# Weights of layers 1 and 2 laid out by partition and both loaded at the front, tile 0's rows written from ACT's queue, layer 2's mixed weights made earlier on DVE

## The chip, the cores and the metric

The kernel runs on one core of a Trainium2 chip. The metric is the device time of one execution in microseconds (us). A core has five engines with their own instruction streams: PE (TensorE, matmul), DVE (VectorE), ACT (ScalarE), POOL (GpSimd) and SP (SyncE, used here for DMA issues only). Sixteen DMA engines move data between HBM (the chip's memory) and SBUF (128 partitions). PSUM is the memory that PE writes.

## The reference, cut to what matters

For 512 samples, 39 embedding rows of 16 numbers each are gathered, and three layers of a "compressed interaction network" are computed on them, followed by a small dense tower.

```python
e = stack([tbl_f[ids[:, f]] for f in range(39)], axis=1)         # (512, 39, 16)
prev = e
for k in range(3):                                               # 128 units each
    h = prev.shape[1]                                            # 39, then 128, 128
    z = einsum('bmd,bhd->bdmh', e, prev).reshape(b, D, m * h)
    t = einsum('bdc,co->bdo', z, w[k]) + bias[k]
    t = transpose(t, (0, 2, 1))
    t = t / sqrt(sum(t * t, axis=(-2, -1), keepdims=True))
    logit.append(t); prev = t
z = sum(concatenate(logit, axis=1), axis=-1)                     # (512, 384)
h = concatenate([z, dense_ctx], axis=1)
h = maximum(h @ W_top1 + b_top1, 0)
h = maximum(h @ W_top2 + b_top2, 0)
y = h @ W_top3
```

w[1] and w[2] have 128 * 39 rows of 128 numbers (2.56 MB each); row m * 128 + h belongs to field m and unit h.

## The kernel before, in words

**Tiling.** The batch is cut into 16 tiles of 32 samples; a tile's data are 32 * 16 = 512 columns. Tile 0 is written out with `first=True`, tiles 1 to 14 are a loop, tile 15 is written out with `last=True`.

**Data path of a tile.** POOL gathers the embedding rows with ten indirect DMAs (L300) into `gathered`. Three DMAs (`write_rows`) write them to `xt` in HBM, where the data have one row per field. POOL also makes `mixed` from them (L316 to L321), and `write_mixed` writes it to `xq` in HBM. From `xt` come `x3` and `xr` (117 partitions, layer 0: `load_x` and `load_shifted`, four groups g of `xr`), and from `xt` and `xq` comes `xb`, whose rows are repeated over all 128 partitions (`load_chunk`).

**Layer 0.** DVE multiplies `x3` (in tile 0 from SBUF, in the others from a copy in PSUM that ACT makes in `copy_x`) into `xr` (`products0`, L625), and PE multiplies with `w0_sb` (L799).

**Layers 1 and 2.** The 39 fields are worked through in 11 chunks c = 0 to 10 (`CHUNKS`). Four are direct chunks "D" (c = 0, 2, 7, 10) with 2 or 3 fields: DVE makes `z` = t * xb (L642) and PE multiplies with the fields' weights (L808). Seven are pair chunks "P" with two pairs of fields: a scheme of the Strassen kind, in which PE makes seven half-size products per pair (L822) instead of eight. It needs sums of parts of `z`, made by POOL (L337, L340) and for two chunks (c = 5 and 6 of layer 1) by DVE (L655) from a copy that ACT makes, and sums of parts of the weights. These "mixed weights" `s_sb[k]` are made once per layer by `mixed_weights(k, part)` on DVE (L612) in four parts, each of a 128x768 and a 128x128 instruction. Part 3 overwrites a quarter of `w_sb[k]` in place. PE waits for all four parts before chunk 0 of the layer in tile 0.

**What sets the order.** Everything is ordered by hand: each engine has one stream, and semaphores hold it. `z` is a ring, so that DVE waits for PE to have used a slot (`z_used`) before it writes it again. Within a tile DVE runs the products of layer 1, c = 0 to 10, then `shared_sums` and `add_shared` (the end of layer 1), then the products of layer 2. PE runs layer 1, layer 0 of the next tile, layer 2. In the loop's tiles DVE makes the next tile's `products0` after chunks 9 and 10 of layer 1 (L745 to L748); in tile 0 it makes them after all of layer 1's chunks (L749 to L753), with parts 1 to 3 of layer 2's mixed weights behind them, and part 0 ahead of chunk 10 (L743).

**The queue of SP.** SP issues, in this order: the small inputs, w0b, w0a, w1 (L372); then the writes of tile 0's rows (`write_rows(0)`), `xq` of tile 0, two of the four groups of `xr`; when all four have landed, the chunk loads of tile 0; in their middle (after c = 5) the writes of tile 1's rows and of `xq` of tile 1; then w2 (L430) and the layer 0 loads of tile 1. ACT's queue issues `x3` and the other two groups of `xr` of tile 0. The lines of the weight loads:

```python
sp.dma_start(w_sb[1][:, :, :], w1.rearrange("(m h) o -> h m o", h=P)).then_inc(w_loaded[1], 16)   # L372
sp.dma_start(w_sb[2][:, :, :], w2.rearrange("(m h) o -> h m o", h=P)).then_inc(w_loaded[2], 16)   # L430
```

Each partition h gets 39 pieces of 512 B, one per field.

Of the kernel before, what the change touches and what calls it, by code (L numbers as in the profile page):

```python
# [127 lines left out]
def build(nc, ids_in, base_in, masks_in, table, xt, xq, dense_t, w0a, w0b, w1, w2, b0, b1, b2,  # L128
          wt1, bt1, wt2, bt2, wt3, out):
    ctx = ExitStack()  # L130
    with ctx:
# [148 lines left out]

        block = ctx.enter_context(nc.Block())
# [84 lines left out]
        def _(sp):  # L366
# [5 lines left out]
            sp.dma_start(w_sb[1][:, :, :], w1.rearrange("(m h) o -> h m o", h=P)).then_inc(w_loaded[1], 16)  # L372

            def write_rows(i):

                def write(first, g0, g1, fields=GROUP):
                    blk = xt[bass.ds(i, 1), first:first + (g1 - g0 - 1) * GROUP + fields, :].rearrange(
                        "a (g f) (b d) -> (a f b) g d", f=fields, d=EMB)
                    sp.dma_start(blk, gathered[0:fields * TILE_B, g0:g1, :]).then_inc(xt_written, 16)

                sp.wait_ge(rows_gathered, 16 * (GROUPS - 1) * (i + 1))
                write(0, 0, GROUPS - 1)
                write(FIELDS, 0, (XT_ROWS - FIELDS) // GROUP)
                sp.wait_ge(last_gathered, 16 * (i + 1))
                write((GROUPS - 1) * GROUP, GROUPS - 1, GROUPS, LAST_GROUP)
# [28 lines left out]
            write_rows(0)  # L414
# [9 lines left out]
            for c in range(NCH):  # L424
                load_chunk(0, c)
                if c == NCH // 2:

                    write_rows(1)
                    write_mixed(1)
            sp.dma_start(w_sb[2][:, :, :], w2.rearrange("(m h) o -> h m o", h=P)).then_inc(w_loaded[2], 16)  # L430
            sp.wait_ge(xt_written, 96)
            sp.wait_ge(acc0_ready, 1)
            load_layer0(1)

# [7 lines left out]
            with sp.Fori(1, TILES - 1) as i:  # L442
                load_fields(i)
                write_rows(i + 1)
# [24 lines left out]
        def _(act):  # L469
# [5 lines left out]

            act.wait_ge(xt_written, 48)
# [112 lines left out]
        def _(dve):  # L589
# [143 lines left out]
            def tile(i, first=False, last=False):  # L733
                for c in range(NCH):
# [39 lines left out]
            products0(0, range(len(LOADS0)))  # L774
# [205 lines left out]
```

## Time and profile before

| what | us |
|---|---|
| device time, median of 3 runs | 1170.16 (1168.98 to 1170.77) |
| device time of the profiled execution | 1173.38 |
| its span, from the first to the last instruction | 1171.6 |
| busy in the span: PE | 1120.3 (96%) |
| DVE | 994.8 (85%) |
| POOL | 946.5 (81%) |
| ACT | 144.6 (12%) |
| mean granted TensorE clock | 0.991 |

Spans and starts are counted in us from the first instruction. A timeline row has the start, the length, the engine (SPq and ACTq: a DMA issue on that queue; PEld: a weight load of PE), the line, the operation, output<-inputs with buffer numbers left out, the form and the count of instructions merged; in brackets stands the idle time of the engine before it and what ended it ("issue": nothing that the profile shows). A window row has the length, then busy time and instruction count of each engine asked for, the granted clock (1.00 is 2.4 GHz, 0.50 is 1.2 GHz), the mean busy share of the 16 DMA engines, and GB/s. Ends of matmuls are modelled, and a share can come out a little above 1.

### The profile page before, as it was taken

The page shows a single profiled execution, that of the slowest core. Times are in us where ns is not written, and L with a number is a line of the kernel's source. Part 1 is how long each engine was busy: PE and PEld are TensorE (multiplying, and loading weights), DVE is VectorE, ACT ScalarE, POOL GpSimd, SP SyncE. Part 2 cuts the span into 40 slices and gives each one's busy share as a digit, 9 for nine tenths or more (in the row PEclk, how much of TensorE's full clock was granted, in tenths as well). Part 3 has the DMA queues.
Part 4 walks back from the last instruction along what each step waited for, and adds up shares of the span by engine and source line. Part 5 has one row for each costly group of instructions (what it writes and reads, how often), then busy time and mean ns, then how long its engine had stood idle before and what let it go on. Part 6 is the DMA issues. An engine that isn't in the chain of part 4 may idle for free. (4 is left out here: it accounts for less than half of the span.)

```text
span 1171.6 us, 22368 instructions
## 1 busy us (share of the span) xinstructions
PE 1120.3 (96%) x8252; PEld 612.8 (52%) x8252; DVE 994.8 (85%) x875; ACT 144.6 (12%) x298; POOL 946.5 (81%) x646
## 2 busy tenths in 40 slices
PE   0788999999999999999999999999999999999999
PEld 0344555555555555555555555555555555555553
DVE  2658989899898989989898998988999898999782
ACT  0001111101111110111111011111101011110102
POOL 5566889798888979898897989889798988958680
PEclk9898999999999999999999999999999999999999
DMA  6886637293653718275472827547282844728010
GB/s 181 252 273 222 200 104 265 67 320 92 241 181 127 251 65 328 75 261 161 143 245 68 318 71 270 152 152 247 72 303 71 284 138 168 236 69 300 1 51 1
DMA packets 102345, 205.81 MB, mean 176 GB/s; under 512 B 49915, under 2 KB 52923, under 8 KB 102326
## 3 DMA queue, kind: packets, MB, share of 16 engines
q1 hardware_dynamic: 95312, 203.29, 51.7%
q0 software_dynamic: 5120, 1.29, 1.1%
q10 hardware_dynamic: 1894, 0.96, 0.4%
q8 instruction: 13, 0.21, 0.1%
q14 instruction: 6, 0.05, 0.0%
HBM read 203.05 MB, written 2.46 MB: 175 GB/s over the span
## 5 line engine op out<-in xcount | busy, mean ns | idle before, releaser
L642 DVE TENSOR_TENSOR z<-t_ps,xb 128x2048 f32<-128x2048 f32 (+2 forms) x352 | 711.1, 2043 | 68.0 <-PE acc L822 43.5
L340 POOL TENSOR_TENSOR sums<-z,sums 128x1024 f32<-128x1024 f32 x224 | 531.6, 2373 | 53.8 <-DVE sums L655 38.7
L808 PE MATMUL acc<-z,w_sb 128*64 128x512 f32 x1408 | 327.6, 601 | 16.5 <-DVE z L642 10.7
L822 PE MATMUL mix_ps<-sums,s_sb 128*64 128x256 f32 x1792 | 330.8, 380 | 2.0 <-POOL sums L340 0.8
L337 POOL TENSOR_TENSOR sums<-z 128x512 f32<-128x512 f32 x192 | 245.7, 1280 | 83.6 <-DVE z L642 79.4
L822 PE MATMUL acc<-z,w_sb 128*64 128x256 f32 x896 | 269.4, 383 | 0.2
L822 PE MATMUL mix_ps<-z,w_sb 128*64 128x256 f32 x896 | 269.4, 383 | 0.0
L822 PE MATMUL acc<-z,s_sb 128*64 128x256 f32 x896 | 267.9, 381 | 0.0
L822 PE MATMUL p_ps<-z,w_sb 128*64 128x256 f32 x896 | 267.9, 381 | 0.0
L822 PEld LDWEIGHTS mix_ps<-sums,s_sb 128*64 128x64 f32 x1792 | 187.2, 137 | 99.3 <-POOL sums L340 13.5
L822 PE MATMUL acc<-sums,w_sb 128*64 128x256 f32 x896 | 230.9, 380 | 0.0
L808 PEld LDWEIGHTS acc<-z,w_sb 128*64 128x64 f32 x1408 | 104.5, 138 | 176.6 <-issue 159.7
L300 POOL DMA_INDIRECT gathered<-in_table,rows_of x160 | 154.0, 962 | 52.6 <-issue 35.7
L822 PEld LDWEIGHTS acc<-z,w_sb 128*64 128x64 f32 x896 | 121.6, 138 | 106.3 <-issue 56.1
L822 PEld LDWEIGHTS acc<-z,s_sb 128*64 128x64 f32 x896 | 123.5, 138 | 61.2 <-issue 1.1
L799 PE MATMUL acc<-xr,w_sb 117*64 117x512 f32 x448 | 103.2, 612 | 28.9 <-DVE xr L625 28.1
L822 PEld LDWEIGHTS p_ps<-z,w_sb 128*64 128x64 f32 x896 | 123.4, 138 | 0.0
L822 PEld LDWEIGHTS mix_ps<-z,w_sb 128*64 128x64 f32 x896 | 121.6, 138 | 0.0
L822 PEld LDWEIGHTS acc<-sums,w_sb 128*64 128x64 f32 x896 | 120.7, 137 | 0.0
L799 PEld LDWEIGHTS acc<-xr,w_sb 117*64 117x64 f32 x448 | 33.7, 141 | 94.9 <-issue 94.6
L625 DVE TENSOR_TENSOR xr<-t_ps,xr 117x1024 f32<-117x1024 f32 (+1 forms) x60 | 62.5, 1082 | 1.4 <-issue 1.3
L525 ACT COPY cross<-mix_ps 64x256 f32<-64x256 f32 x32 | 11.7, 365 | 394.5 <-PE acc L822 264.3
(80 smaller groups left out, 447.7 us busy)
## 6 DMA issues: line engine op xcount, KB each, us to landing
xb<-xt SPq DMA_DIRECT2D x128, 512.0 KB, 6.5
xb<-xq SPq DMA_DIRECT2D x112, 512.0 KB, 5.1
xb<-xt SPq DMA_DIRECT2D x48, 768.0 KB, 6.8
xr<-xt SPq DMA_DIRECT2D x47, 468.0 KB
x<-xt SPq DMA_DIRECT2D x15, 234.0 KB
xr<-xt SPq DMA_DIRECT2D x15, 234.0 KB
gathered<-in_table,rows_of POOLq DMA_INDIRECT x160
xt<-gathered SPq DMA_DIRECT2D x16, 72.0 KB, 2.3
```

The source lines that it names most:

```text
L300: nc.gpsimd.indirect_dma_start(gathered[0:n, g, :], None, table[:, :], bass.IndirectOffsetOnAxis(rows_of[0:n, g:g + 1], 0)).then_inc(rows_ ...
L337: nc.gpsimd.tensor_tensor(t2, t3, b11, ALU.add).then_inc(pool_t2, 1)
L340: nc.gpsimd.tensor_tensor(t41, b2, t2_twice, ALU.subtract).then_inc(t41_ready, 1)
L525: nc.scalar.copy(cross[RIGHT, N2], mix_ps[LEFT, N2]).then_inc(cross_ready, 1)
L625: nc.vector.tensor_tensor(xr[:, k0:k1, :], x.rearrange("p (a n) -> p a n", a=1).broadcast_to([WIDE, k1 - k0, N]), xr[:, k0:k1, :], ALU.mul ...
L642: nc.vector.tensor_tensor(z[:, at:at + n, :], t_ps[k - 1][:, :].rearrange("p (a n) -> p a n", a=1).broadcast_to([P, n, N]), xb[:, XB_ROW[c ...
L799: last = nc.tensor.matmul(acc0[o, :], w0_sb[:, k, o], xr[:, k, :], start=(k == 0), stop=(k == STEPS0 - 1))
L808: last = nc.tensor.matmul(acc[k][o, :], w_sb[k][:, field + r, o], z[:, at + r, :], start=(c == 0 and r == 0), stop=(c == NCH - 1 and r == ...
L822: return nc.tensor.matmul(bank[side, cols], weights, moving, start=start, stop=stop, skip_group_check=True)
```

## The change

- The host lays w1 and w2 out by unit: 128 rows (one per partition) of 39 * 128 numbers, 19,968 B in one piece. The plain copy of them in SBUF is what it was.
- SP issues w1 and w2 one behind the other at the front.
- `write_rows` becomes a function of the queue. Tile 0's three row writes are issued by ACT, in front of its wait for them; the later tiles' by SP as before.
- On SP, `write_mixed(1)` moves from the middle of tile 0's chunk loads to behind the layer 0 loads of tile 1.
- On DVE, layer 2's mixed weights: parts 0 and 1 between the first and the second group of tile 0's `products0`, part 2 after chunk 3 and part 3 after chunk 4 of layer 1 in tile 0.
- On DVE, tile 1's `products0` stand after chunks 9 and 10 of tile 0 as in every other tile.

```diff
+        def write_rows(engine, i):
...
+                engine.dma_start(blk, gathered[0:fields * TILE_B, g0:g1, :]).then_inc(xt_written, 16)
...
-            sp.dma_start(w_sb[1][:, :, :], w1.rearrange("(m h) o -> h m o", h=P)).then_inc(w_loaded[1], 16)
...
+            sp.dma_start(w_sb[1][:, :, :], w1).then_inc(w_loaded[1], 16)
+            sp.dma_start(w_sb[2][:, :, :], w2).then_inc(w_loaded[2], 16)
...
-            write_rows(0)
             write_mixed(0)
...
                 if c == NCH // 2:
 
-                    write_rows(1)
-                    write_mixed(1)
-            sp.dma_start(w_sb[2][:, :, :], w2.rearrange("(m h) o -> h m o", h=P)).then_inc(w_loaded[2], 16)
+                    write_rows(sp, 1)
             sp.wait_ge(xt_written, 96)
             sp.wait_ge(acc0_ready, 1)
             load_layer0(1)
+            write_mixed(1)
...
+            write_rows(act, 0)
             act.wait_ge(xt_written, 48)
...
-                    if c == NCH - 2 and first:
-                        mixed_weights(2, 0)
-                    if c == 9 and not first and not last:
+                    if first and c in (3, 4):
+                        mixed_weights(2, c - 1)
+                    if c == 9 and not last:
                         products0(i + 1, (0, 1, 2,))
-                    if c == 10 and not first and not last:
+                    if c == 10 and not last:
                         products0(i + 1, (3,))
-                if first:
-
-                    products0(i + 1, range(len(LOADS0)))
-                    for part in range(1, 4):
-                        mixed_weights(2, part)
...
-            products0(0, range(len(LOADS0)))
+            products0(0, (0,))
+            for part in range(2):
+                mixed_weights(2, part)
+            products0(0, range(1, len(LOADS0)))
...
+    def by_unit(w):
+        return np.ascontiguousarray(w.reshape(FIELDS, UNITS, UNITS).transpose(1, 0, 2))
...
-        "w1": a["L0_rec_w1"], "w2": a["L0_rec_w2"], "b0": a["L0_rec_b0"], "b1": a["L0_rec_b1"],
+        "w1": by_unit(a["L0_rec_w1"]), "w2": by_unit(a["L0_rec_w2"]), "b0": a["L0_rec_b0"], "b1": a["L0_rec_b1"],
```

DVE's stream at the end of layer 1 in tile 0, before: chunks 8 and 9 (L642), part 0 of the mixed weights (L612), chunk 10, `products0` of tile 1 (L625), parts 1 to 3, and the first of `shared_sums` (L663).

```order
L642 TENSOR_TENSOR z<-t_ps,xb 128x2048 x2
L612 TENSOR_TENSOR s_sb<-w_sb 128x768
L612 TENSOR_TENSOR s_sb<-w_sb 128x128
L642 TENSOR_TENSOR z<-t_ps,xb 128x1536
L625 TENSOR_TENSOR xr<-t_ps,xr 117x1024 x3
L625 TENSOR_TENSOR xr<-t_ps,xr 117x512
L612 TENSOR_TENSOR s_sb<-s_sb,w_sb 128x768
L612 TENSOR_TENSOR s_sb<-s_sb,w_sb 128x128
L612 TENSOR_TENSOR s_sb<-w_sb,s_sb 128x768
L612 TENSOR_TENSOR s_sb<-w_sb,s_sb 128x128
L612 TENSOR_TENSOR w_sb<-w_sb 128x3x4x64
L612 TENSOR_TENSOR w_sb<-w_sb 128x2x64
```

The same place of DVE in the changed kernel:

```order
L642 TENSOR_TENSOR z<-t_ps,xb 128x2048 x2
L625 TENSOR_TENSOR xr<-t_ps,xr 117x1024 x3
L642 TENSOR_TENSOR z<-t_ps,xb 128x1536
L625 TENSOR_TENSOR xr<-t_ps,xr 117x512
L663 TENSOR_TENSOR cross<-cross,mix_ps 64x256
```

Chunk 10 has three instructions of `products0` ahead of it instead of one part of the mixed weights, and nothing of the mixed weights is left at this place. Parts 2 and 3 stand further up in the changed kernel, behind chunk 3 and behind chunk 4 (the first row here is chunk 3, the last is chunk 5):

```order
L642 TENSOR_TENSOR z<-t_ps,xb 128x2048
L612 TENSOR_TENSOR s_sb<-w_sb,s_sb 128x768
L612 TENSOR_TENSOR s_sb<-w_sb,s_sb 128x128
L642 TENSOR_TENSOR z<-t_ps,xb 128x2048
L612 TENSOR_TENSOR w_sb<-w_sb 128x3x4x64
L612 TENSOR_TENSOR w_sb<-w_sb 128x2x64
L642 TENSOR_TENSOR z<-t_ps,xb 128x2048
```

SP's queue from the middle of tile 0's chunk loads on, before (`xb` is a chunk load, L379 the row writes of tile 1, L390 its `xq`, L430 w2, L273 and L279 the layer 0 loads of tile 1):

```order
L379 DMA xt<-gathered 96x16
L390 DMA xq<-mixed 128x4x16
L401 DMA xb<-xq 128x1024
L401 DMA xb<-xt 128x1024
L401 DMA xb<-xt 128x1536
L401 DMA xb<-xq 128x1024
L401 DMA xb<-xt 128x1024
L401 DMA xb<-xq 128x1024
L401 DMA xb<-xt 128x1024
L401 DMA xb<-xt 128x1536
L430 DMA w_sb<-in_w 128x39x128
L273 DMA x<-xt 117x1x512
```

The same place in the changed kernel (`xq` is now L391, a chunk load L402, a row write L286):

```order
L286 DMA xt<-gathered 96x16
L402 DMA xb<-xq 128x1024
L402 DMA xb<-xt 128x1024
L402 DMA xb<-xt 128x1536
L402 DMA xb<-xq 128x1024
L402 DMA xb<-xt 128x1024
L402 DMA xb<-xq 128x1024
L402 DMA xb<-xt 128x1024
L402 DMA xb<-xt 128x1536
L273 DMA x<-xt 117x1x512
L279 DMA xr<-xt 117x1x1024 x3
L279 DMA xr<-xt 117x1x512
```

The wait for `mixed` and the load of w2 are gone from between the row writes of tile 1 and the layer 0 loads of tile 1.

## Rows read from the trace of the kernel before

**Rows 1.** Windows, PE alone: busy (instructions), granted clock, DMA share, GB/s
```profile
44.80:76.20 31.40, 31.36 (x228) 0.91 0.92 288
76.20:82.00 5.80, 0.02 (x2) 0.96 0.88 240
96.30:102.00 5.70, 5.70 (x20) 0.50 0.68 200
```
**Rows 2.** Timeline of PE: end of layer 1 of tile 0, later two loop tiles
```profile
75.84 0.38 PE L822 MATMUL acc<-sums,w_sb 128*64 128x256 f32 x1
82.01 4.21 PE L808 MATMUL acc<-z,w_sb 128*64 128x512 f32 x12 [5.78 <-issue]
86.05 6.17 PE L799 MATMUL acc<-xr,w_sb 117*64 117x512 f32 x28
96.28 1.97 PE L808 MATMUL acc<-z,w_sb 128*64 128x512 f32 x4 [4.06 <-DVE z L642]
...
158.08 2.75 PE L808 MATMUL acc<-z,w_sb 128*64 128x512 f32 x12
166.67 1.89 PE L808 MATMUL acc<-z,w_sb 128*64 128x512 f32 x8
234.77 1.89 PE L808 MATMUL acc<-z,w_sb 128*64 128x512 f32 x8
```
**Rows 3.** Timeline of DVE, layer 1 of tile 0 (c = 4, 5, 9, then its end)
```profile
52.79 2.29 DVE L642 TENSOR_TENSOR z<-t_ps,xb 128x2048 f32<-128x2048 f32 x1 [2.09 <-PE acc L822]
55.37 2.29 DVE L642 TENSOR_TENSOR z<-t_ps,xb 128x2048 f32<-128x2048 f32 x1 [0.28 <-PE acc L808]
...
67.72 2.29 DVE L642 TENSOR_TENSOR z<-t_ps,xb 128x2048 f32<-128x2048 f32 x1 [1.00 <-PE acc L822]
79.12 1.16 DVE L612 TENSOR_TENSOR s_sb<-w_sb 128x768 f32<-128x768 f32 x2 [9.11 <-DMA w_sb<-in_w]
87.59 1.15 DVE L612 TENSOR_TENSOR s_sb<-s_sb,w_sb 128x768 f32<-128x768 f32 x2
```
**Rows 4.** Timeline of DVE, chunk 10 of layer 1 in tile 1
```profile
155.28 1.75 DVE L642 TENSOR_TENSOR z<-t_ps,xb 128x1536 f32<-128x1536 f32 x1
```
**Rows 5.** Timeline, chunk 6 of layer 1 in tile 0: POOL's sums, PE's matmuls (chunks 5, 6)
```profile
64.11 2.36 POOL L340 TENSOR_TENSOR sums<-z,sums 128x1024 f32<-128x1024 f32 x1 [2.51 <-DVE sums L655]
62.85 0.81 PE L822 MATMUL mix_ps<-sums,s_sb 128*64 128x256 f32 x5
65.87 1.08 PE L822 MATMUL mix_ps<-sums,s_sb 128*64 128x256 f32 x5
```
**Rows 6.** Timeline of SP's queue
```profile
18.46 1.66 SPq L379 DMA_DIRECT2D xt<-gathered  x3
51.57 0.37 SPq L390 DMA_DIRECT2D xq<-mixed  x1
58.59 14.73 SPq L273 DMA_DIRECT2D x<-xt  x1
```
**Rows 7.** Windows: PE, PEld, DVE, ACT, POOL busy; clock, DMA share, GB/s (chunk loads, then w2)
```profile
63.00:66.00 3.00, 3.00 (x32) 2.14 (x29) 2.53 (x3) 0.00 (x0) 1.89 (x1) 1.00 1.04 424
72.00:75.00 3.00, 3.00 (x32) 1.99 (x30) 0.00 (x0) 0.00 (x0) 2.43 (x2) 1.00 1.06 293
```
**Rows 8.** Timeline of the front: DVE and POOL
```profile
17.94 1.26 DVE L612 TENSOR_TENSOR s_sb<-w_sb 128x768 f32<-128x768 f32 x2 [7.95 <-DMA w_sb<-in_w]
21.48 0.29 POOL L294 TENSOR_TENSOR rows_of<-ids_sb,base_sb 128x10 int32<-128x10 int32 x1 [1.11 <-DMA xt<-gathered]
26.75 1.23 DVE L625 TENSOR_TENSOR xr<-x,xr 117x1024 f32<-117x1024 f32 x1 [3.84 <-DMA xr<-xt]
30.35 0.94 POOL L300 DMA_INDIRECT gathered<-in_table,rows_of  x1 [0.30 <-issue]
31.25 2.96 DVE L625 TENSOR_TENSOR xr<-x,xr 117x1024 f32<-117x1024 f32 x3 [3.27 <-issue]
31.60 1.70 POOL L300 DMA_INDIRECT gathered<-in_table,rows_of  x1 [0.31 <-issue]
```

More of the change, by code:

```diff
@@ L279, in load_shifted, with write @@
             engine.dma_start(xr[:, k0:k1, :].rearrange("p k n -> p (k n)"), src).then_inc(xr_loaded[g], 16)
+        def write_rows(engine, i):
+            def write(first, g0, g1, fields=GROUP):
+                blk = xt[bass.ds(i, 1), first:first + (g1 - g0 - 1) * GROUP + fields, :].rearrange(
+                    "a (g f) (b d) -> (a f b) g d", f=fields, d=EMB)
+                engine.dma_start(blk, gathered[0:fields * TILE_B, g0:g1, :]).then_inc(xt_written, 16)
+            engine.wait_ge(rows_gathered, 16 * (GROUPS - 1) * (i + 1))
+            write(0, 0, GROUPS - 1)
+            write(FIELDS, 0, (XT_ROWS - FIELDS) // GROUP)
+            engine.wait_ge(last_gathered, 16 * (i + 1))
+            write((GROUPS - 1) * GROUP, GROUPS - 1, GROUPS, LAST_GROUP)
         block = ctx.enter_context(nc.Block())
@@ L371, in _ @@
             sp.dma_start(w0_sb[:, :, :], w0a).then_inc(w0a_loaded, 16)
-            sp.dma_start(w_sb[1][:, :, :], w1.rearrange("(m h) o -> h m o", h=P)).then_inc(w_loaded[1], 16)
[L374 to L385, printed above, removed]
+            sp.dma_start(w_sb[1][:, :, :], w1).then_inc(w_loaded[1], 16)
+            sp.dma_start(w_sb[2][:, :, :], w2).then_inc(w_loaded[2], 16)
             def write_mixed(i):
@@ L443, in _ @@
                 load_fields(i)
-                write_rows(i + 1)
+                write_rows(sp, i + 1)
                 write_mixed(i + 1)
```

## The prediction

> **What bounds the kernel now.** I read the windows first. From 44.8 us on PE is busy nearly all the time, with one hole: [rows 1] show PE at work through 31.4 us of layer 1 of tile 0, then 5.8 us with nothing to do. The timeline of PE [rows 2] adds the second hole: chunk 10 of layer 1 starts at 82.01 after 5.78 us, layer 0 of tile 1 follows, and layer 2 starts at 96.28 after 4.06 us. Then I compared with the loop. There layer 2 of two successive tiles starts at 166.67 and 234.77, 68.10 us apart, with nothing lost in between. So in the loop PE is the bound, and DVE and POOL have room; only time in front of or inside tile 0 can be won. What PE waits for in the holes is in the timeline of DVE [rows 3]: after chunk 9 of layer 1 (67.72, done at 70.01) DVE sits 9.11 us until w2 has landed (79.12), because part 0 of layer 2's mixed weights stands ahead of chunk 10. That is the first hole. The second comes from parts 1 to 3 (from 87.59), 3 * 1.15 us, with tile 1's `products0` ahead of them, all of them ahead of the end of layer 1. SP's queue tells why w2 is late [rows 6]: SP waits until 51.57 for the `mixed` of tile 1, then issues the second half of the chunk loads, w2 after them, and even the issue of `x3` behind w2 takes 14.73 us, a queue full of work.
>
> **The two holes go: 13.9 us.** In the changed kernel chunk 10 has only `products0` ahead of it, as in the loop. The last matmuls of chunk 9 start at 75.84 and follow each other by about 0.2 us, so chunk 10 can start at 76.05. In the loop it is 166.67 - 158.08 = 8.59 us from there to layer 2 [rows 2], which gives 84.64 instead of 96.28: 11.64 us. After the holes PE ran at the lower clock level: granted 0.50 (1.2 GHz) from 96.3 to 102 after 4.06 us of idling [rows 1]. That shows as 166.67 - 96.28 = 70.39 us to the next layer 2, where the loop has 68.10: another 2.29 us. Chunk 10's own low pace (4.21 us for what takes 2.75) is inside the 11.64. Sum 13.93 us, if nothing else is late.
>
> **What is late next inside tile 0: 0.8 us back.** Part 2 after chunk 3 costs nothing: DVE waited 2.09 us for PE ahead of chunk 4 [rows 3], and a part takes 1.16. Part 3 after chunk 4 meets a wait of only 0.28: chunk 5 starts at 52.79 + 2.29 + 1.16 = 56.24 instead of 55.37, 0.87 late. It then delays DVE's sums for chunks 5 and 6, on which POOL's sums wait (64.11 after 2.51 us), and there PE has nothing in hand: its five matmuls on sums take 1.08 us for chunk 6 against 0.81 for chunk 5 [rows 5]. So between 0 and 0.87 reach PE; I take 0.5. Second, three groups of `products0` now stand between chunks 9 and 10. By their lengths (1.23, and 2.96 for three [rows 8]) they take about 3.5 us: 70.01 + 3.5 + 1.75 = 75.3 for the end of chunk 10's `z`, where PE wants it at 76.05. The loop lives with about the same room: 155.28 + 1.75 = 157.03 for 158.08 [rows 2, 4]. But it needs tile 1's `x3` and `xr` by 70 to 73 us. They now follow the chunk loads directly: SP no longer waits for `mixed`, which lets the second half of the chunk loads start up to 3 us sooner, and w2, 2.56 MB / 293 GB/s = 8.7 us of the queue [rows 7], is gone from ahead of them. Before, w2 landed at 79.12 [rows 3] with these loads right behind it; 8.7 plus 3 us sooner puts them at 67.4 and after, just in time. I take 0.3 us, and 3.5 as the upper end (all three groups late by their own length). Together 0.8, bounds 0 and 4.4.
>
> **The front: 1.5 us back.** Layer 0 of tile 0 hangs on the chain gathers, row writes (issued at 18.46 [rows 6]), rows in `xt` (POOL sees them at 21.48), first `products0` at 26.75 [rows 8]. w2 is now moved beside this chain. Rates: rows of 512 B moved at 293 GB/s, pieces of 4 to 6 KB at 424, both with the DMA engines full [rows 7]. Nothing here shows pieces of 19,968 B; I take 424. Then w1 needs 6.0 us instead of 8.7 and lands at about 15.2 instead of 17.94, and w2 6.0 us later, at 21.2. Its last 3 us lie beside the last gathers and the row writes, of small pieces; since ACT's queue issues the writes they don't stand behind w2 but share the engines with it. I take 1.0 us. Then the mixed weights of layer 1 begin at 15.2 and lie beside POOL's last gather instead of behind it. [Rows 8] show what that does: a gather issued while DVE is idle takes 0.94 us, one issued under DVE's instructions on `x3` and `xr` 1.70. One or two of the ten are hit: I take 0.5 of at most 1.5 us. Bounds of the front: -0.5 us (w1's early end lets gathers land sooner) and +5.2. The upper end has both weights at 293 GB/s: w2 lands at 17.94 + 8.7 = 26.7, and SP's half of the `xr` loads stands behind it in the queue, 26.7 - 21.48 = 5.2 us later.
>
> The trace's 1.70 us gather is what the Trainium skill (SBUF — State Buffer, Who interferes with whom) states as a lock: a DVE instruction with two SBUF inputs holds back a GpSimd instruction that reads SBUF, and whoever comes second waits for the other's end. By that rule one part's large instruction holds a gather by up to a whole instruction, here not more than the bound just used. A rule that speaks against the new layout is in DMA: Bandwidth & Descriptors, Specifications: 512 B is given as the smallest transfer for the line rate, so longer rows would bring nothing. The trace does not agree, 293 against 424 GB/s; by that rule the sum would be the first rival's.
>
> Parts 0 and 1 of layer 2 go into the gap behind the first `products0`: 26.75 + 1.23 = 27.98, two parts of 1.26 and 1.16 end at 30.4, the next `products0` was held until 31.25 [rows 8]. Nothing is lost while w2 has landed by 28.8; at 26.7 it still has. `write_mixed(1)` is wanted only in tile 1, and moving it costs nothing.
>
> **Sum.** -13.9 + 0.8 + 1.5 = -11.6 us. The profiled execution took 1173.38 (span 1171.6), which gives 1161.8 for one like it; it lies 3.2 above the median of the runs, 1170.16, which gives 1158.6. A measurement of this kernel can tell about 0.2% (2.3 us) from no change.
>
> **Rivals.**
> - *The longer rows bring no rate.* w1 and w2 together hold the queue until 26.7, tile 0 starts 5.2 us late: -13.9 + 0.8 + 5.2 = -7.9, 1162.3. For it: nothing in the trace moves such pieces. Against it: 424 GB/s at 4 to 6 KB.
> - *The front costs nothing.* w2 is through before the row writes need the engines: -13.9 + 0.8 = -13.1, 1157.1. For it: the row writes are on another queue; against it: small pieces beside a full load.
> - *Layer 0's loads of tile 1 come late.* Chunk 10 stands behind `products0`, so a late `xr` becomes a new hole of PE: 3.5 us and the clock's 2.3 behind it, -13.9 + 0.5 + 1.5 + 5.8 = -6.1, 1164.1. For it: a room of only 0.8 us. Against it: w2's 8.7 us are gone from ahead.
> - *Slower: the two big loads crawl at the front.* If pieces of 19,968 B keep only a third of the engines at work (424 / 3 = 141 GB/s), w1 and w2 take 36 us and w2 lands at about 43. SP's `xr` loads stand behind it: tile 0 starts 43 - 21.5 = 21.5 us late, 1170.16 - 13.1 + 21.5 = 1178.6. It decides from w2 landing at 21.5 + 13.1 = 34.6, that is at under about 180 GB/s. Against it: all loads over 128 partitions in the trace fill the engines.
> - *The change doesn't close the hole*, since DVE or POOL is too late elsewhere in tile 0 and the time is back within 2.3 us of 1170.
>
> **How the numbers follow.** Forecast 0.60, no rate 0.15, free front 0.12, late layer 0 loads 0.08, slower 0.03, no change 0.02. The time is the forecast's, 1158.6. The range goes from the free front with its bound, -13.9 - 0.5 = -14.4 (1155.8), up over the no-rate case with half of the tile 0 bound more, to 1163.5; the late loads' case, the slower one and no change, 13 in 100, lie above. Faster 0.95, same 0.02, slower 0.03.
>
> **What the profile of the changed kernel would show.** The holes: no idle time of PE of more than 1 us between chunk 9 of layer 1 in tile 0 and layer 2, layer 2 of tile 0 at about 86 to 87, and no stretch at clock 0.50 after it; the distance to the next layer 2 is 68.1. The front: DVE's first mixed weights at about 15; w2 landed before 28; first `products0` at 28.3 instead of 26.75 (32 in the no-rate case). Tile 0: chunk 5 of DVE 0.9 us later against PE than before; chunk 10's `z` about 0.5 to 1 us before PE wants it. I am wrong if the first matmul of layer 1 starts more than 5 us later than 44.8, or if PE idles again behind chunk 9.

## The result and the profile after

Before 1170.77 us (1168.98 to 1173.04, 13 runs), after 1164.47 us (1161.53 to 1167.44, 13 runs): ratio 0.9939 with the interval [0.9929, 0.9949], which is 7.1 us less (6.0 to 8.3). Predicted were 11.6 us less, 1158.6, and at most 1163.5. The direction came as forecast, the gain is three fifths of it. The profiled execution took 1164.96 (1173.38 before), its span is 1163.1 (1171.6), 8.5 us less. All times below leave out one execution, of w2_behind_xr, that took 1335.7 us at a granted clock of 0.848, where its others had 0.993 to 0.997.

The two holes are gone. PE at the end of layer 1 of tile 0, windows over PE alone (busy with its instructions, granted clock, DMA share, GB/s):

```profile
48.60:82.00 33.40, 31.45 (x228) 0.91 0.74 249
82.00:90.60 8.60, 8.60 (x44) 1.00 0.25 53
90.60:96.00 5.40, 5.40 (x42) 1.00 0.91 266
```

And PE's timeline there (start, length, instruction; in brackets the idle time before it and what ended it):

```profile
80.77 0.81 PE L820 MATMUL mix_ps<-sums,s_sb 128*64 128x256 f32 x5
82.06 2.75 PE L806 MATMUL acc<-z,w_sb 128*64 128x512 f32 x12
84.64 6.18 PE L797 MATMUL acc<-xr,w_sb 117*64 117x512 f32 x28
90.65 1.89 PE L806 MATMUL acc<-z,w_sb 128*64 128x512 f32 x8
...
158.19 1.89 PE L806 MATMUL acc<-z,w_sb 128*64 128x512 f32 x8
```

Chunk 10 follows chunk 9 without a wait (5.78 us in [rows 2]), it takes 2.75 instead of 4.21, layer 2 starts at 90.65 instead of 96.28, no window stands at clock 0.50 as the third of [rows 1] does, and the next layer 2 comes 67.54 us later, where it was 70.39 (the loop's 68.10 was forecast; why it is 0.56 less is open).

But layer 2 was forecast at 86 to 87. The front gives the first part of the difference. PE and DVE there:

```profile
31.33 3.68 PE L797 MATMUL acc<-xr,w_sb 117*64 117x512 f32 x8 [31.33 <-DVE xr L625]
36.71 6.44 PE L797 MATMUL acc<-xr,w_sb 117*64 117x512 f32 x20 [1.70 <-DVE xr L625]
48.65 1.97 PE L806 MATMUL acc<-z,w_sb 128*64 128x512 f32 x4 [3.67 <-DVE z L642]
```
```profile
14.69 1.16 DVE L612 TENSOR_TENSOR s_sb<-w_sb 128x768 f32<-128x768 f32 x2 [5.15 <-DMA w_sb<-in_w]
29.96 1.22 DVE L625 TENSOR_TENSOR xr<-x,xr 117x1024 f32<-117x1024 f32 x1 [10.52 <-DMA xr<-xt]
31.10 1.15 DVE L612 TENSOR_TENSOR s_sb<-w_sb 128x768 f32<-128x768 f32 x2
32.29 1.21 DVE L612 TENSOR_TENSOR s_sb<-s_sb,w_sb 128x768 f32<-128x768 f32 x2
35.43 2.96 DVE L625 TENSOR_TENSOR xr<-x,xr 117x1024 f32<-117x1024 f32 x3 [1.93 <-DMA xr<-xt]
```

w1 is there at 14.69 (17.94 in [rows 8]; I had 15.2), yet the first `products0` starts at 29.96 instead of 26.75 and layer 1 at 48.65 instead of 44.79. The reason stands on POOL. `masked`, the first step of `mixed`, and the row writes wait for the rows of the first nine gathers. POOL is through with the ninth at 16.67 (15.66 + 1.01) and issues the tenth, then `masked` waits another 3.47 us, and the data are in `xt` at 24.77 (21.48 in [rows 8]).

```profile
15.66 1.01 POOL L313 DMA_INDIRECT gathered<-in_table,rows_of  x1 [0.30 <-issue]
16.97 0.92 POOL L313 DMA_INDIRECT gathered<-in_table,rows_of  x1 [0.30 <-issue]
21.37 0.29 POOL L329 TENSOR_TENSOR masked<-gathered,masks 128x64 f32<-128x64 f32 x1 [3.47 <-DMA gathered<-in_table,rows_of]
24.77 0.20 POOL L307 TENSOR_TENSOR rows_of<-ids_sb,base_sb 128x10 int32<-128x10 int32 x1 [2.47 <-DMA xt<-gathered]
```

The same place in the kernel before:

```profile
16.12 0.92 POOL L300 DMA_INDIRECT gathered<-in_table,rows_of  x1 [0.30 <-issue]
18.52 0.53 POOL L316 TENSOR_TENSOR masked<-gathered,masks 128x64 f32<-128x64 f32 x1 [1.47 <-DMA gathered<-in_table,rows_of]
```

The tenth gather is issued 0.85 us later than before, since one at 8.51 took 1.85 instead of 0.95. That costs nothing: in parts_gap, mixed_back and writes_sp below, with the same loads at the front, no gather is that slow, POOL is through with the ninth at 15.7 to 15.9, and the row writes still start at 21.62 to 21.95.

The windows (here PE, PEld, DVE, ACT, POOL; clock, DMA share, GB/s) show the DMA engines full, faster than the 293 GB/s of the 512 B rows in [rows 7], until w2 ends at about 20 (the window from 19 to 20 has 297 GB/s, the next 10):

```profile
12.00:15.00 3.00, 0.00 (x0) 0.00 (x0) 0.31 (x1) 0.00 (x0) 2.39 (x3) 1.00 0.94 379
15.00:18.00 3.00, 0.00 (x0) 0.00 (x0) 2.93 (x6) 0.00 (x0) 2.29 (x3) 1.00 1.04 418
18.00:21.00 3.00, 0.00 (x0) 0.00 (x0) 1.41 (x4) 0.00 (x0) 0.00 (x0) 1.00 0.57 223
```

The second part of the difference lies inside tile 0. DVE around chunks 3 to 5 of layer 1, and POOL beside it:

```profile
54.48 1.37 DVE L612 TENSOR_TENSOR s_sb<-w_sb,s_sb 128x768 f32<-128x768 f32 x2
56.49 2.29 DVE L642 TENSOR_TENSOR z<-t_ps,xb 128x2048 f32<-128x2048 f32 x1 [0.64 <-PE acc L820]
58.70 3.20 DVE L612 TENSOR_TENSOR w_sb<-w_sb 128x768 f32<-128x768 f32 x2
61.82 2.28 DVE L642 TENSOR_TENSOR z<-t_ps,xb 128x2048 f32<-128x2048 f32 x1
```
```profile
54.70 1.01 POOL L331 TENSOR_TENSOR mixed<-gathered,masks 128x64 f32<-128x64 f32 x1
56.06 1.28 POOL L350 TENSOR_TENSOR sums<-z 128x512 f32<-128x512 f32 x1
57.41 2.38 POOL L353 TENSOR_TENSOR sums<-z,sums 128x1024 f32<-128x1024 f32 x1
59.74 2.00 POOL L350 TENSOR_TENSOR sums<-z 128x512 f32<-128x512 f32 x1
```

Part 3 (58.70), of two instructions, takes 3.20 us where parts 0 and 1 took 1.15 and 1.21, and POOL's 128x512 sum beside it 2.00 instead of 1.28. Chunk 5 follows chunk 4 by 61.82 - 56.49 = 5.33 us instead of 2.58. PE pays for it at the matmuls on sums of the next chunks, where five take 1.15 us instead of the 0.81 at 62.85 in [rows 5], and two are waited for:

```profile
63.53 1.15 PE L820 MATMUL mix_ps<-sums,s_sb 128*64 128x256 f32 x5
68.08 0.43 PE L820 MATMUL mix_ps<-sums,s_sb 128*64 128x256 f32 x1 [0.59 <-POOL sums L353]
72.53 0.43 PE L820 MATMUL mix_ps<-sums,s_sb 128*64 128x256 f32 x1 [1.21 <-POOL sums L353]
```

The account: from the start of layer 1 to layer 2 it is 90.65 - 48.65 = 42.00 us; the prediction's holeless tile 0 has 84.64 - 44.79 = 39.85, so 2.15 us were lost inside. -13.93 (holes and clock) + 3.86 (front) + 2.15 (inside) - 0.56 (67.54 against 68.10) = -8.48, the difference of the spans, 8.5.

### The profile page after: what moved, and what is told of

Its sections match the earlier page's. It is cut to its first block and busy times, and to the rows that moved or that the text cites. A ratio compares the mean times of both kernels' runs of the same rounds, so it can differ in the third digit from the quotient of the medians.

```text
span 1163.1 us, 22368 instructions
## 1 busy us (share of the span) xinstructions
PE 1115.4 (96%) x8252; PEld 608.4 (52%) x8252; DVE 996.0 (86%) x875; ACT 144.3 (12%) x298; POOL 946.5 (81%) x646
## 5 line engine op out<-in xcount | busy, mean ns | idle before, releaser
L642 DVE TENSOR_TENSOR z<-t_ps,xb 128x2048 f32<-128x2048 f32 (+2 forms) x352 | 710.9, 2043 | 66.1 <-PE acc L820 43.8
L353 POOL TENSOR_TENSOR sums<-z,sums 128x1024 f32<-128x1024 f32 x224 | 531.4, 2372 | 54.7 <-DVE sums L655 39.6
L625 DVE TENSOR_TENSOR xr<-t_ps,xr 117x1024 f32<-117x1024 f32 (+1 forms) x60 | 62.3, 1081 | 0.0
L525 ACT COPY cross<-mix_ps 64x256 f32<-64x256 f32 x32 | 11.6, 364 | 405.5 <-PE acc L820 405.5
```

The lines of the kernel that those rows point to most:

```text
L353: nc.gpsimd.tensor_tensor(t41, b2, t2_twice, ALU.subtract).then_inc(t41_ready, 1)
L525: nc.scalar.copy(cross[RIGHT, N2], mix_ps[LEFT, N2]).then_inc(cross_ready, 1)
L625: nc.vector.tensor_tensor(xr[:, k0:k1, :], x.rearrange("p (a n) -> p a n", a=1).broadcast_to([WIDE, k1 - k0, N]), xr[:, k0:k1, :], ALU.mul ...
L642: nc.vector.tensor_tensor(z[:, at:at + n, :], t_ps[k - 1][:, :].rearrange("p (a n) -> p a n", a=1).broadcast_to([P, n, N]), xb[:, XB_ROW[c ...
```

## Experiments

All are compared with the kernel before on the same chip. PE's start of layer 0's second batch (20 matmuls), of layer 1 and of layer 2 in tile 0, with the issue of the row writes and the first `products0`, by the timelines (us):

| kernel | row writes | `products0` | second batch (length) | layer 1 | layer 2 | ratio |
|---|---|---|---|---|---|---|
| before | 18.46 | 26.75 | 32.53 (6.76) | 44.79 | 96.28 | |
| after | 21.37 | 29.96 | 36.71 (6.44) | 48.65 | 90.65 | 0.9939 |
| layout_only | 17.37 | 25.26 | 32.46 (7.45) | 45.40 | 92.62 | 0.9950 |
| rows_512 | 22.01 | 34.05 | 41.99 (6.89) | 54.37 | 96.35 | 0.9969 |
| pieces_4k | 20.33 | 29.06 | 35.38 (6.83) | 47.70 | 89.66 | 0.9912 |
| parts_gap | 21.95 | 30.29 | 37.29 (7.53) | 50.31 | 89.08 | 0.9917 |
| w2_behind_xr | 17.97 | 26.01 | 39.85 (6.71) | 52.06 | 91.69 | 0.9942 |
| pieces_gap | 20.34 | 29.07 | 36.69 (7.49) | 49.67 | 88.42 | 0.9911 |
| mixed_back | 21.70 | 30.30 | 36.57 (4.51) | 46.58 | 89.91 | 0.9948 |
| writes_sp | 21.62 | 29.83 | 36.39 (6.53) | 48.42 | 90.38 | 0.9937 |
| no_w2_load | 17.22 | 25.19 | 32.11 (7.63) | 45.24 | 87.22 | 0.9878 |
| direct_late | 19.22 | 27.50 | 35.25 (6.04) | 46.79 | 87.83 | 0.9920 |
| w2_mid | 17.28 | 25.31 | 31.28 (6.46) | 43.23 | 89.80 | 0.9960 |
| direct_last | 19.03 | 27.29 | 34.94 (7.22) | 47.65 | 88.27 | 0.9897 |

Two of these columns scatter by themselves. The second batch starts 5.8 to 7.9 us behind the first `products0` (13.8 in w2_behind_xr), and its 20 matmuls take 4.51 to 7.63 us. In after 4 of them start in each us until 40, in mixed_back 8 from 37 on; the granted clock reads 1.00 in both all the while, so what slows them at first isn't shown. The front is therefore read by the row writes and the first `products0`.

The inside of tile 0 is read from layer 1 to layer 2. With parts 2 and 3 behind chunks 3 and 4 it takes 41.96 to 42.00 us in five kernels (after, rows_512, pieces_4k, writes_sp, no_w2_load; 42.2 in mixed_back less its wait for chunk 10), whether the granted clock in the 4.8 us from 3.2 us behind the start of layer 1 is 0.70 or 1.00. Without them it depends on that clock: 38.75 to 39.0 at 0.99 and 1.00 (parts_gap, pieces_gap, direct_last less its wait for chunk 10), 39.6 to 39.9 at 0.71 to 0.79 (before without its holes, w2_behind_xr, direct_late less its wait). So the two parts cost 2.1 to 2.4 us at the low clock and 3.0 to 3.2 at the high one.

**layout_only**: the kernel before, with the new layout of w1 and w2 and nothing else.

```diff
-            sp.dma_start(w_sb[2][:, :, :], w2.rearrange("(m h) o -> h m o", h=P)).then_inc(w_loaded[2], 16)
+            sp.dma_start(w_sb[2][:, :, :], w2).then_inc(w_loaded[2], 16)
...
+        "w1": by_unit(a["L0_rec_w1"]), "w2": by_unit(a["L0_rec_w2"]),
```

> The kernel before with the host layout of w1 and w2 by partition and nothing else: w2 stays behind tile 0's chunk loads, all DVE and queue orders are those of before. Theory A (the layout only raises the rate of the two loads): w2 lands about 2.7 us sooner, 76.4 instead of 79.1, the first hole of PE shrinks by that and the clock's part stays; gain 2 to 4 us, 1167 to 1169. Rival (the layout itself slows the front because its large pieces hold up the gathers): the rows of tile 0 land later than 18.5, up to 2 us, and the gain is 0 to 1 us.

Measured 1166.27 us, ratio 0.9950 [0.9937, 0.9964], 5.9 us less; theory A had 1167 to 1169. The row writes start at 17.37, earlier than before: w1 is there at 15.19, before POOL is through with the ninth gather (15.86), so its load in large pieces costs the front nothing. Whether large pieces in flight beside the last gathers slow them can't be read here. The two holes of [rows 2] shrink by themselves, since w2 lands at 75.88 instead of 79.12:

```profile
78.76 4.49 PE L808 MATMUL acc<-z,w_sb 128*64 128x512 f32 x12 [2.70 <-DVE z L642]
92.62 3.34 PE L808 MATMUL acc<-z,w_sb 128*64 128x512 f32 x8 [3.37 <-DVE z L642]
```

By the times the layout alone brings the greater part, and all the moved work adds 1.2 us to it, with intervals that overlap. By the traces it is half: the layer 2 of tile 1 starts 4.2 us sooner than before (162.45 for 166.67), in after 8.5 (158.19); the profiled execution of layout_only, 1169.17, was the slowest of its six.

**rows_512**: the changed kernel with w1 and w2 in their old layout.

```diff
-            sp.dma_start(w_sb[2][:, :, :], w2).then_inc(w_loaded[2], 16)
+            sp.dma_start(w_sb[2][:, :, :], w2.rearrange("(m h) o -> h m o", h=P)).then_inc(w_loaded[2], 16)
```

> The changed kernel with both weights in their old layout, 39 pieces of 512 B a partition, still both at the front. Theory A (it is the size of the pieces that holds up the gathers): the gathers land as in the kernel before, first rows written at about 18.5 to 19.5 although w2 is in flight until about 26; then x3 and xr are late behind w2, tile 0's layer 1 starts at 48 to 50. Rival B (any load that fills the DMA engines delays the gathers alike): rows written at 21 or later, layer 1 of tile 0 starts after 51.

Measured 1168.83 us, 0.9969 [0.9958, 0.9980]. Rival B held. The gathers are as late with 512 B rows (writes at 22.01) as with 19,968 B pieces (21.37 to 21.95), so pieces of this size are not needed for the delay. The loads also run longer here: DVE has w1 at 18.67, and the engines move 256 GB/s or more until 26, so that the rows come while w2 is still in flight, where in after they come 1.4 us behind its end. The row writes themselves now stand beside it, and the rows reach `xt` only at 29.19:

```profile
29.19 0.20 POOL L307 TENSOR_TENSOR rows_of<-ids_sb,base_sb 128x10 int32<-128x10 int32 x1 [5.43 <-DMA xt<-gathered]
```

**pieces_4k**: each weight load in five DMAs of at most 8 fields, 4,096 B per piece.

```diff
+                for m in range(0, FIELDS, 8):
+                    sp.dma_start(w_sb[k][:, m:min(m + 8, FIELDS), :], w[:, m:min(m + 8, FIELDS), :]).then_inc(w_loaded[k], 16)
```

> The changed kernel with each weight load cut into five DMAs of eight fields, 4096 B a partition and piece, the host layout kept. Theory A (size of the pieces): full rate is kept (400 GB/s or more) and the gathers' small pieces wait behind 4 KB instead of 20 KB: rows of tile 0 are written at 18.5 to 20 instead of 21.4, layer 1 of tile 0 starts at 46 to 47 instead of 48.65, total 1.5 to 2.5 us below the changed kernel. Rival B (full engines, whatever the size): rows written at 21 to 21.5 and no change of the time, within 0.5 us.

Measured 1161.22 us, 0.9912 [0.9897, 0.9927]. The rate is 370 to 396 GB/s in the windows of 1 us from 14 to 20. Row writes at 20.33 here and 20.34 in pieces_gap, against 21.37 to 21.95 in the four kernels with the front of after: 1 to 1.6 us of the 3 to 4 come back, between theory A (18.5 to 20) and rival B (21 to 21.5). The Trainium skill (DMA: Bandwidth & Descriptors, SWDGE vs HWDGE vs iDMA) says that a DMA engine serves the two kinds of queue in turn and changes only at packet boundaries; if smaller pieces mean smaller packets, which it doesn't say, gathers would get in sooner. The trace agrees for 4 KB (`masked` waits 3.16 us, in mixed_back 4.69), but not for the 512 B rows above (4.91), so what holds the gathers inside the DMA engines stays open.

**parts_gap**: parts 2 and 3 of layer 2's mixed weights behind tile 0's last `products0`.

```diff
-                    if first and c in (3, 4):
-                        mixed_weights(2, c - 1)
...
             products0(0, range(1, len(LOADS0)))
+            for part in range(2, 4):
+                mixed_weights(2, part)
```

> The changed kernel with parts 2 and 3 of layer 2's mixed weights made on DVE directly behind tile 0's products0, where DVE was idle for 5.5 us, instead of after chunks 3 and 4. Theory C (DVE's instructions of part 3 stood for POOL's, 3.2 us instead of 1.16, and the delay went through the sums of chunks 5 and 6 to PE): PE's waits for POOL in tile 0 (0.6 and 1.2 us) go, layer 1 of tile 0 takes 1.8 to 2.2 us less, total 1162.3 to 1162.8 where the changed kernel has 1164.5. Rival D (POOL itself is late in tile 0, with or without the parts): the waits of 0.6 and 1.2 us stay and the time is that of the changed kernel.

Measured 1162.61 us, 0.9917 [0.9904, 0.9930]. Theory C held. From layer 1 to layer 2 it is 38.77 us, 3.23 less than in after and 1.08 less than before without its holes; the 1.08 go with the clock (0.99 against 0.71 in the stretch named above), the other 2.15 with the parts. The part of the same shape takes 1.16 again, and POOL's sum 1.27:

```profile
38.89 1.15 DVE L612 TENSOR_TENSOR s_sb<-w_sb,s_sb 128x768 f32<-128x768 f32 x2
40.08 1.16 DVE L612 TENSOR_TENSOR w_sb<-w_sb 128x768 f32<-128x768 f32 x2
57.42 2.29 DVE L642 TENSOR_TENSOR z<-t_ps,xb 128x2048 f32<-128x2048 f32 x1 [1.19 <-PE acc L820]
```
```profile
60.71 1.27 POOL L350 TENSOR_TENSOR sums<-z 128x512 f32<-128x512 f32 x1
```

The waits of PE from 48 to 92 us (in total, times, longest) show what is left, in parts_gap and then in after:

```profile
PE mix_ps L820 <- POOL sums L353: 0.2, 1, 0.2
```
```profile
PE mix_ps L820 <- POOL sums L353: 1.8, 2, 1.2
```

**w2_behind_xr**: w2 behind SP's two `xr` loads of tile 0, all four parts behind `products0`.

```diff
-            sp.dma_start(w_sb[2][:, :, :], w2).then_inc(w_loaded[2], 16)
...
             load_shifted(sp, 0, 2)
+            sp.dma_start(w_sb[2][:, :, :], w2).then_inc(w_loaded[2], 16)
```

> The changed kernel with w2 issued by SP behind its two xr loads of tile 0 instead of in front of the gathers' landing, and all four parts of layer 2's mixed weights on DVE behind tile 0's products0. Theory E (w2 beside w1 and the gathers costs the front 3 to 5 us): tile 0's rows are written at 17.4 as in the run with the layout alone, first products0 at 25 to 26; w2 fills the DMA engines while xr lands, lands at 35 to 37, the parts end before 42; layer 1 of tile 0 starts at 45 to 47 instead of 48.65 to 50.3, total 1158 to 1160. Rival F (the weight traffic costs the same wherever it stands before tile 0's layer 1): the xr loads on ACT's queue are late by what the rows gain, layer 1 starts at 48 to 50, total 1161 to 1163.

Measured 1165.33 us, 0.9942 [0.9927, 0.9956], above both ranges. The row writes are early again (17.97), the first `products0` too. But the second group of `xr` stands on ACT's queue, issued at 22.38, and w2 on SP's at 22.86 runs beside it; DVE waits for it:

```profile
26.01 1.22 DVE L625 TENSOR_TENSOR xr<-x,xr 117x1024 f32<-117x1024 f32 x1 [6.30 <-DMA xr<-xt]
38.57 2.36 DVE L625 TENSOR_TENSOR xr<-x,xr 117x1024 f32<-117x1024 f32 x2 [11.33 <-DMA xr<-xt]
```

The place only moves the cost, to a later link of the same chain.

**pieces_gap**: pieces_4k and parts_gap together.

```diff
+                for m in range(0, FIELDS, 8):
...
+            for part in range(2, 4):
+                mixed_weights(2, part)
```

> Both edits of the first series together: pieces of 4096 B at the front, and parts 2 and 3 behind tile 0's products0. If the gain of the pieces is real (front 1 to 2 us sooner) it adds to that of the parts: 1159 to 1160.5. If it was scatter of the front between executions (48.65 and 50.31 were seen in two kernels with the same front), the time is that of the run with the parts alone, 1161.5 to 1163.

Measured 1162.00 us, 0.9911 [0.9894, 0.9929]: from layer 1 to layer 2 38.75 us, as in parts_gap, and row writes as in pieces_4k. But the second group of `products0` starts at 35.41 (35.43 in after, 34.10 in pieces_4k), so the second batch is no earlier than in after. The time is the rival's (1161.5 to 1163) and can't be told from either alone; that the two gains add up isn't shown.

**mixed_back**: `write_mixed(1)` in the middle of the chunk loads again.

```diff
                     write_rows(sp, 1)
+                    write_mixed(1)
...
             load_layer0(1)
-            write_mixed(1)
```

> The changed kernel with the write of tile 1's mixed rows back in the middle of tile 0's chunk loads. Theory G (moving it is what lets x3 and xr of tile 1 land in time): SP waits for mixed until about 56, chunks 6 to 10 and then x3 land 3 to 4 us later (x3 at 74 instead of 70.6, xr after it), products0 at 75.9 waits, chunk 10 comes late and PE idles 1 to 4 us: total 1 to 5 us above the changed kernel. Rival H (my step: it costs nothing where it stands, the rest of the queue has room without w2): within 0.7 us of the changed kernel.

Measured 1166.70 us (1161.55 to 1169.59), 0.9948 [0.9930, 0.9965], inside the scatter of after, so the times decide for neither theory. The trace does tell: the layer 0 loads of tile 1 are issued 2.4 us later (`xr` at 61.22 instead of 58.83), and chunk 10 waits for `products0`, which waits for them:

```profile
74.11 1.23 DVE L625 TENSOR_TENSOR xr<-t_ps,xr 117x1024 f32<-117x1024 f32 x1 [0.17 <-DMA xr<-xt]
75.66 1.23 DVE L625 TENSOR_TENSOR xr<-t_ps,xr 117x1024 f32<-117x1024 f32 x1 [0.33 <-DMA xr<-xt]
78.33 1.23 DVE L625 TENSOR_TENSOR xr<-t_ps,xr 117x1024 f32<-117x1024 f32 x1 [1.45 <-DMA xr<-xt]
```
```profile
81.27 2.80 PE L806 MATMUL acc<-z,w_sb 128*64 128x512 f32 x12 [1.13 <-DVE z L642]
```

**writes_sp**: tile 0's row writes on SP's queue as before.

```diff
-            write_rows(act, 0)
...
+            write_rows(sp, 0)
             write_mixed(0)
```

> The changed kernel with tile 0's three row writes issued by SP behind w2 instead of by ACT. The trace of the changed kernel has w2 landed at about 21 and the writes issued at 21.4, so the queue in front of them is empty: no change of the time (within 0.7 us), rows landed at 24 to 25 as before. Rival: the separate queue was needed, rows land 1 us or more later and the time rises by that.

Measured 1164.66 us, 0.9937 [0.9923, 0.9952], every time of the front within 0.4 us of after: the queue that issues them doesn't matter here, where w2 has ended (about 20) before they are issued.

**no_w2_load**: w2 isn't loaded; DVE fills its place with a constant at the start, so layer 2 computes with that instead of w2.

```diff
-            sp.dma_start(w_sb[2][:, :, :], w2).then_inc(w_loaded[2], 16)
...
+            nc.vector.memset(w_sb[2][:, :, :], 0.01).then_inc(w_loaded[2], 16)
             dve.wait_ge(w0a_loaded, 16)
```

> The changed kernel without the load of w2: DVE fills its place with a constant at the start, where it idles, so layer 2 is computed with wrong weights; every other instruction stays. It prices w2's traffic at the front by itself. Theory E (w2 beside w1 and the gathers costs the front about 4 us): rows written at 17.4 to 18.5, second batch of layer 0's matmuls in tile 0 at 32.5 instead of 36.7, total 3.5 to 4.5 us below the changed kernel, 1160 to 1161. Rival (the front is late because w1's load in large pieces and DVE's earlier mixed weights hold up the gathers): rows stay at 21 and the gain is under 1.5 us.

Measured 1158.76 us, 0.9878 [0.9864, 0.9892]. `masked` waits 0.26 us behind the tenth gather, where it was 3.47 in after and 4.68 to 4.69 in parts_gap, mixed_back and writes_sp. It starts 1.5 us after POOL is through with the ninth gather (14.77 + 0.95), against 4.7 to 6.0 in those four:

```profile
14.77 0.95 POOL L313 DMA_INDIRECT gathered<-in_table,rows_of  x1 [0.30 <-issue]
16.02 0.92 POOL L313 DMA_INDIRECT gathered<-in_table,rows_of  x1 [0.30 <-issue]
17.21 0.29 POOL L329 TENSOR_TENSOR masked<-gathered,masks 128x64 f32<-128x64 f32 x1 [0.26 <-DMA gathered<-in_table,rows_of]
```
```profile
32.11 7.63 PE L797 MATMUL acc<-xr,w_sb 117*64 117x512 f32 x20 [1.87 <-DVE xr L624]
```

The row writes start at 17.22, 4.2 us sooner than in after, and PE's second batch at 32.11, 4.6 us sooner and as early as before (32.53). So w2's traffic is the whole cost of the front. The gain in time, 5.7 us by the medians, is more than the 3.5 to 4.5 expected; the profiled execution (1161.23) was the slowest of the four.

**direct_late**: parts_gap, and the fields 30 to 38 of w1 and w2, 9 of 39, not at the front but among the chunk loads.

```diff
+            sp.dma_start(w_sb[1][:, 0:30, :], w1[:, 0:30, :]).then_inc(w_loaded[1], 16)
+            sp.dma_start(w_sb[2][:, 0:30, :], w2[:, 0:30, :]).then_inc(w_loaded[2], 16)
...
+                if c == 0:
+                    sp.dma_start(w_sb[1][:, 30:39, :], w1[:, 30:39, :]).then_inc(w_late[1], 16)
                 if c == NCH // 2:
+                    sp.dma_start(w_sb[2][:, 30:39, :], w2[:, 30:39, :]).then_inc(w_late[2], 16)
```

> The kernel with parts 2 and 3 behind tile 0's products0 (label parts_gap), and in addition only fields 0 to 29 of both weights at the front (all that the mixed weights need); fields 30 to 38 of w1 are loaded behind tile 0's first chunk load and those of w2 in the middle of the chunk loads. That takes 1.18 of 5.11 MB of weights away from the gathers. Theory E in proportion: a quarter of the front's 4 us, 0.7 to 1.3 us sooner than parts_gap, 1160.5 to 1161.5. Rival (the gathers are late whenever both loads are there, not in proportion to their bytes): as parts_gap, 1162 to 1162.6.

Measured 1161.88 us, 0.9920 [0.9906, 0.9935]. A quarter less to load brings the row writes to 19.22 and layer 2 to 87.83, but `xr` of tile 1 is late for DVE (0.95, 0.72 and 0.25 us), and PE waits 1.10 us for chunk 10. The time lies between theory E (up to 1161.5) and the rival (from 1162).

**w2_mid**: all of w2 in the middle of the chunk loads, all four parts behind chunk 10.

```diff
-            sp.dma_start(w_sb[2][:, :, :], w2).then_inc(w_loaded[2], 16)
...
                 if c == NCH // 2:
+                    sp.dma_start(w_sb[2][:, :, :], w2).then_inc(w_loaded[2], 16)
```

> The changed kernel with w2's load in the middle of tile 0's chunk loads (ahead of the row writes of tile 1) and all four parts of layer 2's mixed weights on DVE right behind tile 1's products0, when POOL makes no sums. Front as with the layout alone: layer 1 of tile 0 starts at 45 to 46. The parts delay the end of layer 1: DVE's first product of layer 2 ends about 3.8 us later than in the loop, PE idles 1.5 to 2.5 us ahead of layer 2 and runs the next stretch partly at the lower clock. Layer 2 of tile 0 starts at 87.5 to 88.5 (90.65 in the changed kernel, 89.1 in parts_gap), total 1161 to 1163. If w2 between the chunk loads makes x3 and xr of tile 1 late, chunk 10 waits too and the total is 1164 to 1166.

Measured 1167.30 us, 0.9960 [0.9947, 0.9973]. Expected were 1161 to 1163, or 1164 to 1166 with late loads of tile 1. Layer 1 starts earliest of all (43.23), and it is lost again: DVE waits 3.33 us for a chunk load, and PE behind it 3.2 us in all for POOL's sums; `xr` of tile 1 is late by 0.67, 0.37 and 1.58 us, and PE waits 1.79 us for chunk 10 and 1.70 for layer 2.

**direct_last**: direct_late with the rest of w2 behind the layer 0 loads of tile 1.

```diff
-                    sp.dma_start(w_sb[2][:, 30:39, :], w2[:, 30:39, :]).then_inc(w_late[2], 16)
...
             load_layer0(1)
+            sp.dma_start(w_sb[2][:, 30:39, :], w2[:, 30:39, :]).then_inc(w_late[2], 16)
```

> The kernel with label direct_late, with fields 30 to 38 of w2 loaded behind tile 1's layer 0 loads instead of in the middle of tile 0's chunk loads. In direct_late the front was 2.7 us sooner than in the changed kernel (rows written at 19.2), but tile 1's x3 and xr were late and chunk 10 cost PE 1.1 us. If that wait was the moved 0.59 MB, it goes: layer 2 of tile 0 starts at about 86.7 to 87.3, total 1160 to 1161. If it was the front's earlier start that left the queue too little time before tile 1's products0 (rows of tile 1, then 4.7 MB of chunks), the wait stays at 0.5 us or more and the total is that of direct_late, 1161.5 to 1162.5.

Measured 1161.28 us (1160.66 to 1162.41), 0.9897 [0.9883, 0.9911], 12.1 us less than before: by ratio the best version that loads w2, and faster than both kernels. Its interval overlaps those of pieces_4k, pieces_gap and parts_gap. The time lies between the two expectations. The wait for `xr` did not go, and PE waits 1.63 us for chunk 10:

```profile
72.45 1.23 DVE L629 TENSOR_TENSOR xr<-t_ps,xr 117x1024 f32<-117x1024 f32 x1 [0.66 <-DMA xr<-xt]
74.46 1.22 DVE L629 TENSOR_TENSOR xr<-t_ps,xr 117x1024 f32<-117x1024 f32 x1 [0.78 <-DMA xr<-xt]
76.69 1.22 DVE L629 TENSOR_TENSOR xr<-t_ps,xr 117x1024 f32<-117x1024 f32 x1 [1.01 <-DMA xr<-xt]
```

So it wasn't w2's rest ahead of these loads. Two reasons are left, and neither was tried by itself: since the front is earlier, the queue has less time for the same chunk loads before tile 1's `xr` is wanted, and w1's rest still stands ahead of them.

## Why the prediction was partly right

Two terms of the sum were too small: the front, put at 1.5 us, measured 3.9, and the inside of tile 0, put at 0.8, measured 2.15. The mechanism of the gain and that of the inside were right.

- *"The two holes go: 13.9 us."* Right: no wait of PE between chunk 9 and layer 2, the low clock behind it gone, next layer 2 after 67.54 us (68.1 forecast).
- *"What is late next inside tile 0: 0.8 us back."* The mechanism was right (part 3 delays DVE's sums, POOL's sums behind them, and PE has nothing in hand), its size wrong: 2.15 us. I priced part 3 at the 1.16 it takes when POOL is idle or gathering. Beside POOL's sums it took 3.20. That neighbours on DVE and POOL lengthen each other was in [rows 8], the gather of 1.70 us, and I used it for gathers only. parts_gap, which moves parts 2 and 3, takes PE's waits for POOL from 1.8 us to 0.2, and the kernels without the two parts there need 2.1 to 2.4 us less from layer 1 to layer 2 at the same low clock. That they collide at the memory's port is the Trainium skill's reading (SBUF — State Buffer, Who interferes with whom); what the runs show is that both engines lengthen together, and that they don't where the parts stand elsewhere. The second term, chunk 10's room, was right, and cost nothing where I took 0.3: `z` ends at 79.33 + 1.75 = 81.08 for PE at 82.06, and `xr` of tile 1 is never waited for.
- *"The front: 1.5 us back."* This step failed most: the row writes came 2.9 us late, the first `products0` 3.2, layer 1 3.9. Its first half was right (w1 at 14.69 for 15.2, at 379 GB/s and more). The half about small transfers was not: I let w2's last 3 us cost them 1.0 us in all. In fact the rows of the gathers come 3.2 to 4.5 us later after the ninth gather than without w2 (4.7 to 6.0 against 1.5; before, with w1 until 17.94, it was 2.6), and everything behind them follows. no_w2_load takes the whole cost away, layout_only shows that w1's load in the same layout costs nothing, and rows_512 that the delay doesn't need large pieces. The 0.5 us for mixed weights under a gather was not seen in after (0.92 to 1.01 us for the gathers from 15.66 on), where one gather at 8.51 took 1.85 beside DVE's addition to w0. In w2_behind_xr and direct_last one gather beside them did take 1.69 and 1.68; in the first the row writes came at 17.97, 0.6 to 0.75 later than in layout_only and no_w2_load.
- *"Parts 0 and 1 go into the gap: nothing is lost."* Right, at 31.10 to 33.50 while DVE waits until 35.43.
- *"Moving write_mixed(1) costs nothing."* Right, but I missed what it earns: by mixed_back about 1.1 us of PE's wait. I had used it only for the start of the chunk loads.
- Rivals: the front was nearest to "the longer rows bring no rate" (3.9 us of its 5.2), but not in cause. "Late layer 0 loads" has the nearest time, 1164.1; that is chance, since in after nothing waited for them. "Crawl" and "not closed" didn't occur either. My sign of being wrong, layer 1 over 5 us late, did not show although the front failed: it was set too wide.
- Two sums don't close. In the crawl rival w1 starts at 9.2 by the forecast's own 15.2 - 6.0, and w2 would land at 45, not 43. The range's upper end, by its words 1162.3 and half of 4.4 more, is 1164.5, or 1163.7 with the 0.8 taken out; I wrote 1163.5.
- In the profiled execution the sum was off by 2.4 (front) + 1.35 (inside) - 0.56 = 3.2 us, which is 1164.96 - 1161.8. The medians are 5.9 apart; the rest, 2.7 us, is in how the profiled executions stand to their medians (before 2.6 above 1170.77, after 0.5 above 1164.47) and in the first three runs of before lying 0.6 lower.

## What to carry to other kernels

Before a large load is moved to an "idle" stretch, list the small transfers on the critical chain of that stretch: each pays for the full DMA engines, also from another queue (POOL's gathers and ACT's `xr` load were late beside a load on SP's), and moving the load behind one of them charges the next. A DVE instruction has two prices, one beside an idle POOL and one beside a busy one; take the second where POOL's own result is wanted next. Try the parts of a change alone: here a new layout without any moved instruction had half of the gain or more.

## What the runs showed of the hardware that I had not expected

- The rows of small gathers arrive 4.7 to 6.0 us after POOL is through with them beside a load that fills the DMA engines, 1.5 without it, and neither 512 B rows nor 4,096 B pieces cure it (writes at 17.22 without w2; with it 22.01, 20.33 and, at 19,968 B, 21.37).
- With full engines the rate goes with the row length: 293 GB/s at 512 B [rows 7], 256 to 292 at the front of rows_512, 370 to 396 at 4,096 B, 379 to 418 at 19,968 B.
- Two instructions of DVE took 3.20 us instead of 1.16 beside POOL's sums, a larger factor (2.8) than that of the gather in [rows 8] (1.70 for 0.94, 1.8).
- A gather that POOL issues 0.06 to 0.09 us behind the start of a DVE instruction of about 1 us took 1.68 to 1.85 us instead of 0.94 (after at 8.51, w2_behind_xr at 14.77, direct_last at 13.55). Where the gather came first, as before at 8.51 with DVE at 8.90, it took 0.95.
- The same 20 matmuls of layer 0 took 4.51 us in one kernel and 7.63 in another, which moves the start of layer 1 by up to 3 us, while the granted clock read 1.00 in both. In mixed_back the early start was kept up to layer 2 (less its 1.13 us of waiting); in parts_gap 1.1 us of a late one were regained at a higher granted clock in layer 1.
